# The one-hots of two edge passes: counting row in PSUM, built two visits sooner

## The reference

```python
# layer 0, part 1 (4 heads): attention over incoming edges, with self loops
logits = leaky_relu(a_src[src] + a_dst[dst]);  alpha = segment_softmax(logits, dst)
x1 = segment_sum(h[src] * alpha, dst)
# layer 0, part 2 (1 head): dot products of queries and keys
alpha2 = segment_softmax((q[dst] * k[src]).sum(-1) / 16, dst)
out = segment_sum(v[src] * alpha2, dst)
# layer 1 (8 heads): two edge types, edge weights
alpha = leaky_relu((x_src[src] * att_src[etype]).sum(-1) + (x_dst[dst] * att_dst[etype]).sum(-1))
a = exp(alpha - segment_max(alpha)[dst]) / denom[dst] * edge_weight
out = segment_sum(x_src[src] * a, dst)
```

## Time and profile before

| | us |
|---|---|
| median of 3 runs | 4023.07 (4012.54 to 4028.57) |
| the profiled execution, its own time | 4020.69 |
| its span, first to last instruction | 4018.8 |
| DMA moved 560.27 MB, mean | 139 GB/s |
| mean granted TensorE clock, share of full speed | 0.854 |

### The profile page before, as it was taken

The page is one execution under the profiler, slowest core; times in us unless marked ns, Lnnn a source line. Parts: engine busy times, 40 slices in busy tenths (PEclk is TensorE's granted clock), DMA queues, the critical chain, the costliest instruction groups (busy, mean ns, idle before and its releaser), DMA issues. The chain is left out here.

```text
span 4018.8 us, 70607 instructions
## 1 busy us (share of the span) xinstructions
PE 2935.1 (73%) x14389; PEld 2089.2 (52%) x14389; DVE 3088.3 (77%) x9652; ACT 1446.3 (36%) x4590; POOL 2729.9 (68%) x2963
## 2 busy tenths in 40 slices
PE   5456666677777677788888888466676677777998
PEld 4334444444455455555555556334444444447998
DVE  6567777788897666677777769678888899997886
ACT  2322233233326456666666666211111111112332
POOL 3577777777750277777777735577777777755886
PEclk8677777778878889999999989677778878888999
DMA  4555555555534444444444437555555555533221
GB/s 131 164 158 163 162 159 161 173 165 169 173 106 120 138 135 136 136 140 137 141 141 141 142 87 221 166 143 147 145 144 147 149 149 149 151 102 92 72 72 50
DMA packets 271620, 560.27 MB, mean 139 GB/s; under 512 B 62118, under 2 KB 164558, under 8 KB 271278
## 3 DMA queue, kind: packets, MB, share of 16 engines
q0 software_dynamic: 115872, 326.30, 29.0%
q10 hardware_dynamic: 82742, 167.20, 13.3%
q1 hardware_dynamic: 72664, 63.00, 5.4%
HBM read 478.39 MB, written 77.89 MB: 138 GB/s over the span
## 5 line engine op out<-in xcount | busy, mean ns | idle before, releaser
L475 PE MATMUL psum<-big,onehots_or_distances 128*128 128x264 f32 (+2 forms) x5280 | 1851.1, 476 | 101.9 <-DVE big L656 55.4
L475 PEld LDWEIGHTS psum<-big,onehots_or_distances 128*128 128x128 f32 x5280 | 1008.2, 223 | 281.2 <-DVE big L656 82.4
L284 POOL DMA_INDIRECT big<-table_attn,src_by_edge x782 | 741.5, 948 | 437.2 <-issue 238.0
L284 POOL DMA_INDIRECT big<-table_typed,src_by_edge x782 | 786.8, 1006 | 249.8 <-issue 237.9
L284 POOL DMA_INDIRECT big<-table_gat,src_by_edge x782 | 783.3, 1002 | 252.6 <-issue 231.8
L341 ACT ACTIVATE dot_products<-big 128x8 f32 (+1 forms) x880 | 156.5, 213 | 1562.1 <-SPq L274 1483.1
L679 DVE TENSOR_TENSOR acc<-acc,psum 128x264 f32 (+2 forms) x1320 | 558.5, 423 | 105.9 <-issue 58.6
L656 DVE TENSOR_TENSOR big<-big,psum 128x512 f32<-128x512 f32 x880 | 594.1, 675 | 14.1 <-issue 4.9
L438 PE MATMUL psum<-big,onehot_t 128*128 x2640 | 462.8, 285 | 155.1 <-SPq L274 91.7
L521 DVE SCALAR_TENSOR_TENSOR dot_products<-psum,big 128x258 f32<-128x258 f32 x880 | 367.6, 421 | 191.0 <-PE psum L438 186.4
L438 PEld LDWEIGHTS psum<-big,onehot_t 128*128 128x128 bf16 x2640 | 260.9, 101 | 362.0 <-issue 247.0
(11 more groups left out here) (284 smaller groups left out, 4243.8 us busy)
## 6 DMA issues: line engine op xcount, KB each, us to landing
onehot_t<-onehots ACTq DMA_DIRECT2D x73, 512.0 KB, 3.8
big<-visit_positions ACTq DMA_DIRECT2D x55, 512.0 KB
onehots<-big ACTq DMA_DIRECT2D x37, 512.0 KB, 5.9
big<-onehots ACTq DMA_DIRECT2D x37, 512.0 KB, 3.6
big<-in_x_dram SPq DMA_DIRECT2D x98, 128.0 KB, 2.7
big<-table_gat,src_by_edge POOLq DMA_INDIRECT x782
big<-table_attn,src_by_edge POOLq DMA_INDIRECT x782
big<-table_typed,src_by_edge POOLq DMA_INDIRECT x782
```

Of the source, the lines that this page charges most:

```text
L284: pool.indirect_dma_start(X[:, t % RING, :], None, ph.table, bass.IndirectOffsetOnAxis(ap=m.src[:, t:t + 1], axis=0)).then_inc(S[f"rows{t ...
L475: last = nc.tensor.matmul(sum_ps(w), onehot_at(v), rows, start=(v % 2 == 0), stop=(v % 2 == 1))
```

## The change

In the first and third pass, VectorE copies the counting row once, at the start of the pass, to the last 128 columns of PSUM bank 3 (`counting`). `onehots` compares against this copy; the positions and the output stay in SBUF. The call for group j moves from visit 4j-2, behind `scale_rows`, to visit 4j-4, ahead of `scale_rows` and of `source_logits`; the first group is built at visit -32. The second pass is as before.

```diff
@@ edge_pass @@
     grow_ps = ps[:, 6, 2 * P:2 * P + H]
+    counting = ps[:, 3, 3 * P:4 * P]
...
                 at = 4 * j % ONEHOTS
-                nc.vector.tensor_tensor(m.onehots[:, at:at + 4, :], m.iota[:, :].unsqueeze(1).to_broadcast([P, 4, P]),
+                nc.vector.tensor_tensor(m.onehots[:, at:at + 4, :], counting.unsqueeze(1).to_broadcast([P, 4, P]),
                                         column(k, 0)[:, g:g + 4].unsqueeze(2).to_broadcast([P, 4, P]), ALU.is_equal).then_inc(S["onehots"], 1)
...
-            dve.wait_ge(S["cleared"], 2)
+            if not ph.dot:
+                nc.vector.tensor_copy(counting, m.iota[:, :]).then_inc(S["cleared"], 1)
+            dve.wait_ge(S["cleared"], 2 if ph.dot else 3)
...
                     places = places_of(DVE_ENGINE, u // 2, PAIRS)
+                if not ph.dot and v % 4 == 0 and 0 < v + 4 < VISIT_END:
+                    onehots((v + 4) // 4)
+                if not ph.dot and v == -2 * G:
+                    onehots(0)
                 if not ph.dot and v % 2 == 0 and 0 <= w + 1 < PAIR_END and (w + 1) % PAIRS:
                     scale_rows(w + 1)
...
                     dot(v + DOT_AHEAD)
-                if not ph.dot and v % 4 == 2 and 0 <= v + 2 < VISIT_END:
-                    onehots((v + 2) // 4)
```

## The result

The changed kernel takes 3977.96 us (median of 4 runs, 3977.29 to 3980.72) against 4024.8 before (4 runs): a ratio of 0.989, 95% interval 0.9868 to 0.9912. It is faster by 47 us; 80 were forecast, and 3977.96 lies above the range. The profiled execution took 3977.4 us (span 3975.5), 43.3 less than that of before.

The account below looks back on a forecast made before the run. GpSimd, running gathers back to back, was taken to set the pace. Gains of 42 + 37 + 1 = 80 us from the profiled 4020.7 gave 3940.7, and 2.4 more for the median 3943 us; range 3920 to 3970.

Parts of the forecast that it names:

- The lock: First and third pass: the all-SBUF comparison holds gathers at their start; reading PSUM removes the stretch, 41.8 and 45.3 us.
- first two steps: Opening readings: GpSimd's gathers set the pace, some stretched by the comparison; with the counting row in PSUM the stretch goes.
- Term 1: First pass, GpSimd: gathers lose 41.8 us of stretch, the 10.6 us of ring waits stay, VectorE follows; gain 42.
- Rival A: First pass: rows come late, each fourth quarter waits 0.5 us more, 25 us come back; 3968 us, chance 0.15.
- Term 2: Third pass, GpSimd: gathers lose 45.3 us, but VectorE itself is late in the last 400 us; gain 37.
- Term 3: The comparison in both passes, with one operand in PSUM, costs what it did, median 678 ns against 679; 0.
- Term 4: One-hot groups built at visit 4j-4 wait for nothing new; gain 1 us, bounds a gain of 2 and a loss of 9.
- Term 5: The added counting-row copy per pass and first group at visit -32 fall into VectorE's 10.8 us wait before tails; 0.
- The sign that the prediction had named: For Term 4: right if TensorE's waits on the comparison vanish and those on the scaling don't grow by as much.
- the three cases that are faster: Whole kernel: the forecast (0.66), Rival A (0.15) and both window differences arriving in full (3930 us, 0.10); given as 0.92.

Follow-up runs that it names:

- e1: Changed kernel with the counting row back in SBUF and no copy, so only the early place of the comparison remains: 4029.8 us.
- e4: Changed kernel with comparisons at their old places in both passes, the third pass's group before a new batch standing behind the edge weights: 3975.7 us.
- e5: Changed kernel with the old places of e4 and LAG 8 for 9: 3944.4 us.
- e7: Changed kernel with the load of the next batch's ring places into VectorE's registers moved from visit 16m-1 to 16m-4, behind the one-hot group: 3966.5 us.
- e3: Changed kernel with the first pass's comparison back at visit 4j-2, still against PSUM; the third pass keeps the early place: 3978.1 us.
- e2: Changed kernel with LAG 8 for 9, so SyncE announces a ring quarter free one quarter earlier: 3952.1 us.
- e6: The kernel before the change with LAG 8 for 9 alone: 4016.6 us.

## Why the prediction was wrong

- *The lock* (first two steps): right. The stretch of 43.3 and 46.0 us is gone, and e1 shows that the place brought none of the gain. The traces say it gather by gather: in the first pass before, 149 gathers began while a comparison ran and took 1233 ns in the mean; in the changed kernel 114 did and took 945, the longest 949.
- *Term 1, first pass, gain 42:* measured 13. The step that failed is "the 10.6 us of ring waits I leave: rows that land late cause them, not VectorE". The cause was named rightly, but not that its price would stay. GpSimd waits for the part of a landing's delay that exceeds the next four gathers, 5.0 us. Of the landings that GpSimd can wait for, 14 were later than that in the kernel before, by 4.3 us in all, and the ring waits beyond the usual 0.3 us gap came to 4.6; in the changed kernel 28 were, by 31.4 us in all, and these waits came to 32.2. So 27.6 of the 43.3 us went there, and 2.7 behind the last gather. Most of it is that the landings themselves became later (4.87 to 5.64 us in the mean of the late ones). The lost stretch as slack is the small part: the four gathers behind a late landing had taken 5.13 us in the mean and take 5.00 now. Why the landings come later stays open. Rival A put the price at 25 us, with a chance of 0.15; its time, 3968, is still 10 too low, as it left terms 2 and 4 as they were.
- *Term 2, third pass, gain 37:* measured 27.8. That rows would no longer hold VectorE in the last 400 us was read rightly from the earlier trace rows; what VectorE's own slowness takes was put at 8 us and is 18 (5.7 in ring waits, 12.6 behind the last gather). A part of that is term 4. With VectorE's batch back at 17.05 us the pass gains 31.4 (e4) and 33.9 (e5, LAG 8), so the term itself was too high by 3 to 6 us. The 37.7 of e7 agree with it only by luck, as its batch is shorter than that of the kernel before.
- *Term 3, the comparison:* right, median 682 ns against 679; the estimate from the Trainium skill's errata (VectorE: DVE Perf Modes, "The TRN2 errata") of 65 ns more isn't borne out.
- *Term 4, the early place, gain 1:* wrong in sign. It looked at semaphores, TensorE and the scaling 0.6 us later, and never at the register load between the group and the scaling, which the group had hidden. The early place costs 0.5 us in a batch of the first pass and 0.3 in the third. In the whole time that is 5 us with the lock in place (e1), can't be told from nothing without it at LAG 9 (e3, e4), and is 3 to 8 us at LAG 8 (e5 against e2); covering the load brings more, 7 to 12 us (e7). The sign that the prediction had named for a failure of this term was there: TensorE's waits on the comparison went (1.9 and 2.0 us), but those on the scaling grew from 26.5 to 40.4 us in the first pass and from 26.2 to 44.1 in the third; in e7 they are 16.9 and 16.4.
- *Term 5:* right; the first group at visit -32 waits for its table (6.4 us, 2 times), inside VectorE's wait for rows.
- *The chances:* the three cases that are faster sum to 0.91, not 0.92.

## What to carry over

When an engine that sets the pace gets faster, don't carry its present waits over as they are, even where the engine that gets faster doesn't cause them: a wait of 10 us became 41. When an instruction is moved, ask what ran on the sequencer in its shadow: register loads have no row in the list of semaphores, but show as "issue" before the next instruction. Parts that depend on one another are seen only in pairs (LAG 8 alone: 3 us, with the lock gone: 26).

## What the runs showed of the hardware

- A gather whose start lay under an all-SBUF `tensor_tensor` of 681 ns took up to 1.48 us, and one of 1.57 us had the comparison start 0.07 us after it. With one operand of the comparison in PSUM no gather exceeded 1.13 (L285 against the earlier trace rows), and none that began under a comparison 0.95:

```profile
L285 POOL DMA_INDIRECT big<-table_gat,src_by_edge x782: 940/946/1127, 145.7 to 1154.7; - x196
```

  That is the rule of the Trainium skill, SBUF — State Buffer, "Who interferes with whom"; the trace agrees for the gather's start, while a comparison 0.58 us into it held nothing. The size of the hold comes out of the trace too: in the median of the 117 held gathers of the first pass the excess is what the comparison had left to run 0.12 us after the gather's start. The six that began in a comparison's last 0.12 us were not held, nor, for a reason that stays open, were 13 that began within 0.02 us of a comparison's start.
- With two transfers of 512 KB issued 0.4 us apart once a batch, the rows of 40 of 196 quarters landed over 4 us behind their last gather, 5.6 in the mean; with the two eight visits apart 8 did. Why the same pair delays rows more in some kernels than in others (4.87 us before, 5.04 in e6, 5.28 in e1, 5.37 in e2, 5.64 in the changed kernel) stays open.
